# Layer 0 of a two-layer kernel rewritten: fewer VectorE and GpSimd instructions, gates kept in PSUM, a new order on every engine, and a third stack for layer 1

## The reference

```
# layer 0
ctx   = ema(x, tau_ctx)                         # h_t = a h_(t-1) + x_t
gated = x * sigmoid([x, ctx] @ Wg.T + bg)
mod   = 0.5 + sigmoid(gelu(x @ Wn1.T + bn1) @ Wn2.T + bn2)      # 32 columns
temporal = sum_d softmax(blend)[d] * ema(gated * mod[d], tau[d])  # d = 0..31
gate  = sigmoid(temporal @ Wtemp.T + btemp)
soma  = gelu(x @ Wsoma.T + bsoma)
x     = x + layernorm((soma * gate) @ Wout.T) * gamma + beta
# layer 1: 16 heads of 8 channels, each row sparse (32 listed keys) or dense with a bias
q, k, v = x @ Wq.T + bq, x @ Wk.T + bk, x @ Wv.T + bv
x = x + softmax(q k.T * scale + bias) v @ Wo.T + bo
```

## Time and profile before

| | |
|---|---|
| three runs, us | 369.98, 377.15, 368.16 |
| profiled execution, us | 366.06 |
| its span, us | 364.3 |
| granted TensorE clock, mean | 0.959 |
| busy: PE, DVE, POOL, ACT | 311.9 (86%), 296.9 (82%), 236.9 (65%), 213.2 (59%) |
| busiest groups | POOL L1411 130.1, DVE L1285 113.8, ACT L934 69.7, PE L669 69.1 |
| DMA | 18.91 MB, 192 of the issues are stack parts of 64 KB |

### The profile page before, as it was taken

How to read it: one execution, slowest core, us unless ns; L and a number is a source line. 1 busy time by engine, 2 the same in 40 slices (tenths; PEclk the granted TensorE clock), 3 DMA queues, 4 the chain that set the end, 5 groups by cost and what they waited for, 6 DMA issues and landing times. The chain is left out here.

```text
span 364.3 us, 10344 instructions
## 1 busy us (share of the span) xinstructions
PE 311.9 (86%) x3351; PEld 213.7 (59%) x3361; DVE 296.9 (82%) x1530; ACT 213.2 (59%) x452; POOL 236.9 (65%) x281
## 2 busy tenths in 40 slices
PE   1769559998999989898938499899899989999994
PEld 0425227565564746564524466777687768777772
DVE  4775997979797878879784877799799989999971
ACT  5833201565646364554705367787688868888772
POOL 2045143464655566564733497699899999999980
PEclk9969788999999999999978989999999999999998
DMA  7101000101001035100552004425544564454011
GB/s 206 48 0 31 0 0 2 30 4 29 2 0 31 3 87 94 20 0 0 74 70 32 0 4 86 91 62 71 141 102 98 82 131 104 98 78 103 3 31 30
DMA packets 23473, 18.91 MB, mean 52 GB/s; under 512 B 2304, under 2 KB 23040, under 8 KB 23424
## 3 DMA queue, kind: packets, MB, share of 16 engines
q1 hardware_dynamic: 23424, 18.31, 25.0%
HBM read 3.62 MB, written 2.10 MB: 16 GB/s over the span
## 5 line engine op out<-in xcount | busy, mean ns | idle before, releaser
L1411 POOL TENSOR_TENSOR arena<-arena,neg_max 128x512 f32<-128x512 f32 x128 | 130.1, 1050 | 21.5 <-DVE neg_max L1285 21.2
L1285 DVE CUSTOM_DVE_ANT_0 arena<-ps,arena 128x128 f32<-128x128 f32 x512 | 113.8, 286 | 13.4 <-PE ps L655 7.5
L934 ACT ACTIVATE arena<-ps 128x512 f32<-128x512 f32 x128 | 69.7, 596 | 16.3 <-PE ps L669 16.3
L669 PE MATMUL ps<-ident_sb,arena 128*128 128x128 f32 x512 | 69.1, 279 | 0.0
L1371 POOL TENSOR_TENSOR arena<-arena 128x448 f32<-128x448 f32 (+6 forms) x56 | 41.8, 746 | 29.9 <-DVE arena L1113 27.4
L669 PEld LDWEIGHTS ps<-ident_sb,arena 128*128 128x128 f32 x512 | 57.0, 142 | 6.6 <-issue 4.2
L1358 POOL TENSOR_TENSOR arena<-decay_a,arena 128x192 f32<-128x192 f32 x32 | 22.3, 717 | 38.5 <-ACT arena L794 38.5
L1285 DVE DVE_READ_ACCUMULATOR2_ANT neg_max<- 128x1 f32 x512 | 42.5, 83 | 0.0
L685 PE MATMUL ps<-arena 128*32 128x128 f32 x1024 | 41.5, 280 | 0.0
L1113 DVE TENSOR_TENSOR arena<-ps,arena 128x448 f32<-128x448 f32 (+6 forms) x56 | 23.5, 426 | 14.2 <-PE ps L456 8.7
L655 PE MATMUL ps<-arena 48*128 48x128 bf16 x512 | 25.7, 220 | 8.3 <-DVE neg_max L1285 5.7
(11 more groups left out here) (154 smaller groups left out, 594.5 us busy)
## 6 DMA issues: line engine op xcount, KB each, us to landing
arena<-q_parts SPq DMA_DIRECT2D x96, 64.0 KB
arena<-k_parts SPq DMA_DIRECT2D x96, 64.0 KB
arena<-in_x SPq DMA_DIRECT2D x8, 256.0 KB, 2.8
out<-arena SPq DMA_DIRECT2D x8, 256.0 KB, 3.0
w_sb<-in_w SPq DMA_DIRECT2D x1, 576.0 KB, 6.5
arena<-in_consts SPq DMA_DIRECT2D x1, 420.0 KB, 5.5
rows_sb<-in_rows SPq DMA_DIRECT2D x1, 288.5 KB, 3.0
ident_sb<-in_ident SPq DMA_DIRECT2D x1, 64.0 KB, 3.1
```

The source lines that it names most:

```text
L669: mm = pe.transpose(ps[1][:, q % 2, k * P:k * P + P], neg_t[q % NT_RING][:, k * P:k * P + P], ident)
L934: act.activation(probT[q % PT_RING], ps[1][:, q % 2, :], ACT.Exp, scale=-1.0)\
L1285: dve.tensor_tensor_reduce(out=neg_t[q % NT_RING][:, cs], in0=ps[0][:, score_bank(c) + slot, cs], in1=nbias[n % 2], scale=1.0, scalar=3.0e ...
L1411: pool.tensor_tensor(t4, t4, neg_max[:, n % 2, 4 * z:4 * z + 4].unsqueeze(2).broadcast_to([P, 4, P]), ALU.subtract).then_inc(s["shifted"], 1)
```

## The change

- **x twice from memory.** A transposed copy of x (`xt`, laid out on the host) is loaded straight into `xT`; `f_x` on TensorE and ScalarE goes. x is also loaded into `xb`, in place of GpSimd's x + beta; beta goes into the bias of `x1T` and into `kept`, which is added to the residual kept for the end. The values' bias goes there too, by way of Wo.
- **SyncE.** `load_x` now issues three loads: xn after the context matmuls, xT after the cross matmuls, xb after the residual, all of group m-2. There are three stacks. The third lies over xb, acc, x1g and x1T.
- **Modulation.** Wn2 is not spread over four zero-padded matrices; four matmuls of 32 rows write in two halves to two banks. VectorE's two tensor-scalars (L1089, L1090) go: ScalarE copies the tanh itself to bf16, and the constant part of 0.5 tanh + 1 becomes `lag_c`, added inside each lag product.
- **Gates in PSUM.** Both tanh activations write back into their PSUM bank, and VectorE's products read them there.
- **Values** are copied to `v_all` by ScalarE instead of VectorE.
- **Order** of every engine's step, below; the one-hots are spread over steps 0 and 1; q and k change places.
- **Prologue.** The weights come in two loads, three loads are issued by ScalarE, the lag weights are made in two halves, and two constant matmuls are new.

```diff
@@ sync
+                                   (w_sb[:, W_FIRST:, :], w[:, W_FIRST:, :], "w_rest_loaded"),
...
             def load_x(i, m):
                 sp.wait_ge(s["ctx_ps"], grp(i, m, 1, -1))
-                sp.wait_ge(s["xb_ready"], grp(i, m, 1, -1))
                 sp.dma_start(by_row(xn[m % 2]), x_v[:, group_rows(i, m), :]).then_inc(s[f"x_loaded{m % 2}"], 16)
+                sp.wait_ge(s["cross_ps"], grp(i, m, 1, -1))
+                sp.dma_start(by_row(xT[m % 2]), xt[:, group_rows(i, m), :]).then_inc(s[f"xT_loaded{m % 2}"], 16)
+                sp.wait_ge(s["x1_ready"], grp(i, m, 1, -1))
+                sp.dma_start(by_row(xb[m % 2]), x_v[:, group_rows(i, m), :]).then_inc(s[f"xb_loaded{m % 2}"], 16)
...
             sp.wait_ge(s["part3_ready"], 2)
+            sp.wait_ge(s["counts_ps"], 1)
             load_stack(0)
             sp.wait_ge(s["cross_ps"], G - 1)
             sp.wait_ge(s["part3_ready"], 4)
             load_stack(1)
-            for g in range(2, G):
-                if g >= 3:
-                    store(g - 3)
-                sp.wait_ge(s["score_ps"], NB2 * (g - 1))
-                sp.wait_ge(s["part3_ready"], 2 * (g + 1))
+            sp.wait_ge(s["v_stored"], G)
+            sp.wait_ge(s["x1b_ready"], G)
+            sp.wait_ge(s["part3_ready"], 6)
+            load_stack(2)
+            for g in range(3, G):
+                sp.wait_ge(s["score_ps"], NB2 * (g - 2))
                 load_stack(g)
+                store(g - 3)
@@ tensor
+            def constants():
+                pe.wait_ge(s["vec_step"], vec("blend_4"))
+                pe.transpose(bank(1, 0)[:, 0:P], bl_4, ident).then_inc(s["blend_turned"], 1)
+                pe.wait_ge(s["w_rest_loaded"], 16)
+                pe.matmul(bank(1, 2)[:, 0:P], col["bv"].broadcast_to([P, P]), wt["wo"], start=True, stop=True)\
+                    .then_inc(s["const_ps"], 1)
+            def lag_constants():
+                pe.wait_ge(s["vec_step"], vec("half_bw"))
+                pe.wait_ge(s["act_step"], scal("apow"))
+                pe.matmul(bank(1, 1)[:, 0:Q], half_bw[0:D, :], apow[0:D, :], start=True, stop=True)\
+                    .then_inc(s["const_ps"], 1)
             def front(i, m):
+                f_hidden(i, m)
+                f_soma(i, m)
+                f_modulation(i, m, 0)
+                f_gate_x(i, m)
+                constants()
+                f_modulation(i, m, 1)
+                f_context(i, m)          # now waits for modT_tanh
+                lag_constants()
+                f_gate_ctx(i, m)
+                f_modulation_n(i, m)
+                f_lags(i, m, range(0, 2))
+                f_gated(i, m)
+                f_lags(i, m, range(2, Q))
             def step(i, m):              # closes: from step 1 on
+                f_hidden(i, m + 1); b_carries(i, m)
+                f_modulation(i, m + 1, 0); f_gate_x(i, m + 1); f_modulation(i, m + 1, 1)
+                f_soma(i, m + 1); f_context(i, m + 1); b_locals(i, m)
+                f_modulation_n(i, m + 1); f_gate_ctx(i, m + 1); c_x1T(i, m - 1)
+                f_lags(i, m + 1, range(0, 2)); c_k(i, m - 1); b_cross(i, m)
+                f_gated(i, m + 1); c_less(i, m - 1, 1, 0); f_lags(i, m + 1, range(2, 3))
+                b_crossT(i, m); f_lags(i, m + 1, range(3, 4)); c_q(i, m - 1); b_gate(i, m)
+                c_less(i, m - 1, 1, 1); c_less(i, m - 1, 0, 0); f_lags(i, m + 1, range(4, 6))
+                c_less(i, m - 1, 0, 1); f_lags(i, m + 1, range(6, 7))
+                b_out(i, m); c_v(i, m - 1); f_lags(i, m + 1, range(7, Q))
+                # the count matmuls: end of step 1 (were: end of step 0)
@@ scalar
+                f_hidden(i, m + 1); f_modulation(i, m + 1); f_mod_part1(i, m + 1)
+                f_soma(i, m + 1); f_context(i, m + 1); f_mod_part1b(i, m + 1)
+                f_modulation_n(i, m + 1); f_gate(i, m + 1)
+                c_x1T(i, m - 1); c_part(i, m - 1, 1, 0); b_cross(i, m); f_gated(i, m + 1)
+                c_part(i, m - 1, 1, 1); c_part(i, m - 1, 0, 0); b_gate(i, m)
+                c_part(i, m - 1, 1, 2); c_part(i, m - 1, 0, 1); c_part(i, m - 1, 0, 2)
+                c_values(i, m - 1)
@@ vector
+            dve.wait_ge(s["const_ps"], 2)
+            dve.wait_ge(s["rows_loaded"], 16)
+            pro("lag_c", dve.tensor_copy(lag_c[:], bank(1, 1)[:, 0:Q]), waited=False)
...
             def f_mod_parts(i, m):
-                dve.tensor_scalar(modT[u], thd[u], 0.5, 1.0, ALU.mult, ALU.add).then_inc(s["modT_ready"], 1)
-                dve.tensor_scalar(mod_pa[u][:], thd[u], 0.5, 1.0, ALU.mult, ALU.add).then_inc(s["mod_part1"], 1)
...
             def f_lags(i, m, lags):
-                    dve.tensor_tensor(packed(prod[u][lag % 2], lag), chunks(bank(u, lag % 2), 0, Q - lag),
-                                      chunks(gT[u], 0, Q - lag), ALU.mult).then_inc(s["prod_ready"], 1)
+                    dve.scalar_tensor_tensor(packed(prod[u][lag % 2], lag), chunks(bank(u, lag % 2), 0, Q - lag),
+                                             lag_c[:, lag:lag + 1], chunks(gT[u], 0, Q - lag), ALU.add, ALU.mult)\
+                        .then_inc(s["prod_ready"], 1)
...
             def front(i, m):
+                lag_weights(0)
+                f_mod_parts(i, m)
                 f_gated(i, m)
-                f_modulation(i, m)
-                f_lags(i, m, range(Q))
+                f_lags(i, m, range(0, 2))
+                lag_weights(1)
+                f_lags(i, m, range(2, Q))
             def step(i, m):              # closes: from step 1 on; opens: steps 0 and 1
+                b_carries(i, m); c_residual(i, m - 1); neighbours()   # the last in step 0 only
+                f_mod_parts(i, m + 1); b_locals(i, m); f_gated(i, m + 1)
+                f_lags(i, m + 1, range(0, 2)); b_temporal(i, m)
+                f_lags(i, m + 1, range(2, 3)); one_hots(first, first + 4)
+                f_lags(i, m + 1, range(3, 4)); one_hots(first + 4, first + 8)
+                b_mixed(i, m); f_lags(i, m + 1, range(4, 5)); one_hots(first + 8, first + 12)
+                f_lags(i, m + 1, range(5, 6)); one_hots(first + 12, first + 16)
+                f_lags(i, m + 1, range(6, 7)); c_moments(i, m)
+                f_lags(i, m + 1, range(7, Q)); c_centre(i, m)         # then late_tables in step 1
@@ gpsimd
             def step(i, m):
-                f_inputs(i, m + 1)
+                f_decayed(i, m + 1, range(GB))
                 c_keep(i, m - 1)
-                f_accumulate(i, m + 1)
+                f_lags(i, m + 1, range(1, Q))
                 c_rstd(i, m)
```

More of the change, by code:

```diff
@@ L80, in scal, with build @@
     return ACT_STEPS.index(name) + 1
-def build(nc, x, w, wn2, cols, rows, consts, ident_in, idx, masks, out):
+def build(nc, x, xt, w, wn2, cols, rows, consts, ident_in, idx, masks, out):
     with ExitStack() as ctx:
@@ L103, in build @@
         rows_sb = sb("rows_sb", [P, R_END])
-        gamma, beta, bo, bv = [rows_sb[:, k * P:k * P + P] for k in range(4)]
+        gamma, beta, bo = [rows_sb[:, k * P:k * P + P] for k in range(3)]
         lt = sb("lt", [P, P])
@@ L159, in build @@
             xT.append(four[:, 0:W])
-            th.append(four[:, W:2 * W])
             ctxT.append(four[:, 2 * W:3 * W])
@@ L166, in build @@
             h1T.append(take(P))
-            modT.append(take(W))
             gT.append(take(W))
@@ L171, in build @@
             modn.append(take(P))
-            weights_at = at[0] - 5 * W - P
+            weights_at = at[0] - 4 * W - P
         xn = [take(W) for _ in range(2)]
-        xb, acc, x1g = [[take(W)] for _ in range(3)]
-        for bufs in (xb, acc, x1g):
-            bufs.append(take(W))
-        one_hot = arena[:, at[0]:at[0] + K_SPARSE * P // 2].bitcast(BF16).rearrange("p (j k) -> p j k", k=P)
+        third_at = at[0]
+        xb, acc, x1g = [[take(W) for _ in range(2)] for _ in range(3)]
         x1T = take(W)
+        take(W)
         def stack_at(n):
@@ L411, in f_hidden, with f_modulation @@
                                    start=True, stop=True)
                 mm.then_inc(s["h1_ps"], 1)
-            def f_modulation(i, m):
+            def f_modulation(i, m, half):
                 u = m % 2
-                pe.wait_ge(s["h1_ready"], grp(i, m, 1, 1))
-                if at_start(i, m, 1):
-                    pe.wait_ge(s["vec_step"], vec(f"wn2_row{GB - 1}"))
-                for b in range(GB):
-                    mm = pe.matmul(bank(u, 1)[:, b * P:b * P + P], wn2_row[:, b, :], h1T[u], start=True, stop=True)
-                mm.then_inc(s["modT_ps"], 1)
+                if half == 0:
+                    pe.wait_ge(s["h1_ready"], grp(i, m, 1, 1))
+                    if at_start(i, m, 1):
+                        pe.wait_ge(s["wn2_loaded"], 16)
+                    if not at_start(i, m, 2):
+                        pe.wait_ge(s["temporal_ready"], grp(i, m, 1, -1))
+                else:
+                    pe.wait_ge(s["modT_half"], grp(i, m, 1, 1))
```

(22 more changed lines are left out.)

427 lines of the change are left out of this document (222 added, 205 removed).

## The result

The kernel after takes 402.76 us (median of four runs, 398.15 to 404.77). Its ratio to the kernel before is 1.087 (95% interval 1.069 to 1.106), so it is 8.7% slower. The forecast was 376, with 385 as its upper end. The profiled execution took 402.22 us with a span of 400.3, against 364.3: 36.0 us more, where 7.1 was forecast.

A forecast was written before the change was run, and what follows sets the result against it. It took a VectorE–TensorE loop to bound the steps, and late stack loads to stall attention. Third stack landing at 249.9, 2.0 clock, the remaining time less 2.7 of waits, and 1.0 gave 371.4; rescaled, 376 us, range 364 to 385.

The forecast's parts named there:

- The sign and the mechanism: Whole kernel: slower, 376 us against 369.98, with late stack loads stalling octets 0 and 16 and a slow clock afterwards.
- Both waits and their clock: TensorE stalls 4.2 us before octet 0 and 8.8 before octet 16, then loses 2.0 to the slow clock.
- The first ends landing ... 18.1 us after its start: SyncE's stack loads: each costs 18 to 21 us; 18.1 taken for the first stack, 19.3 for the third.
- A loop between VectorE and TensorE: Steps 2 to 6: bounded by this loop with little slack, not one full engine; from 20.25 to 19.5 us each.
- Rival 3: Whole kernel longer: steps stay at 20.3, clock takes 3.4, later loads 1 us late each; 382 profiled, 4% slower; 18%.
- 0.94 us less TensorE work a step: Steps 2 to 6: TensorE drops 0.44 us of x transposes and about 0.5 of modulation matmuls, which only cover.
- The prologue (31.0, bounds up to 32.5): Before step 0: gain 1.3 us, loss 2.9, so step 0 starts at 31.0 instead of 29.45; bounds 28.5 to 32.5.
- the three loads issued by ScalarE at the start, where it waits for VectorE anyway: Start of the prologue: ScalarE's issuing of three loads costed at nothing.
- the chain to the constants: Prologue: gelus, TensorE's first half and constants, tanh and context put the constants near 16.0, where weights started at 13.51.
- the halving: Prologue: lag weights' second half, 2.95 us, sits between lag 1 and lag 2 with TensorE and GpSimd behind it.
- Steps 0 and 1: Layer 0's first two steps: sixteen one-hots, 6.0 us, move to step 1; the pair goes from 50.9 to 48.9.
- Octets 0 to 11: Attention's start: 50.2 to 48.1 us, from VectorE's carries beginning 1.35 us earlier and one copy less, 0.68.

The follow-up runs named there:

- run with small loads first: On the version with first stack early and two stacks, ScalarE's three starting loads moved to SyncE's queue behind two small ones: step 0 at 35.60 us, was 38.51.
- The table run: On the version with first stack early and two stacks: counts first among late tables, ScalarE's logarithm between q and k parts; steps 2 and 3 together 42.6 us.
- the fastest version: Kernel after with early first stack, small loads first, reordered tables, unhalved early lag weights, third stack used only when free: span 360.2 us, 0.970 of kernel before.
- the run with the halves together: On the version with first stack early and two stacks, both modulation matmul halves precede the gate's x part: steps 4 to 6 took 20.03, 20.5, 20.0 us.

## Why the forecast was wrong, step by step

**The sign and the mechanism were right.** The first stack behind SyncE's last x load, the third behind the stored values, the slow clock behind the gap (277.91 to the next scores 4.1 us at 0.50), no such wait in later groups: each is in the trace. Undoing one took its wait away and left the other (the runs with the first stack early and with two stacks). Both waits and their clock are about 26 us of the 36; I had 15. The runs won back less, 18 to 21, since two stacks bring waits of 6.1 us in later groups.

**"The first ends landing ... 18.1 us after its start" was mis-sized, and it sized both stalls.** It measured 23.7 and 24.1. For the first stack part of that is chance: the same load took 20.5 in the run with two stacks. I took the two loads of before whose ends I had rows for, the shorter for the first stack and what I called the middle for the third (the middle of 18.1 and 21.0 is 19.55, not 19.3). The trace had the other case: the load issued at 171.87 moved 71 GB/s where 1.57 MB in 18.1 us is 87, and was still going at 195. Window of the kernel before:

```profile
173.00:195.00 22.00, 15.61 (x117) 9.00 (x117) 16.38 (x53) 7.75 (x16) 12.84 (x17) 0.84 0.56 71
```

Nobody waited for it, so no wait pointed at it. The upper bound should have been 24 to 25 us, which gives stalls of 10 and 14.

**"A loop between VectorE and TensorE" was wrong as the bound of steps 2 to 6**, and with it 19.5 us. Doubling a TensorE pair costs a step 0.9 us, doubling a VectorE subtraction in the loop 0.15. Rival 3 had this part right: "steps stay at 20.3". I counted 0.94 us less TensorE work a step as cover. It did not go away. Windows of the step from 100.66 before and of the one from 130.46 after, in the columns of the earlier trace rows:

```profile
100.66:120.73 20.07, 19.04 (x140) 11.75 (x140) 16.96 (x42) 10.58 (x18) 11.78 (x15) 1.00 0.05 14
...
130.46:150.61 20.15, 19.15 (x135) 11.06 (x137) 15.64 (x40) 11.25 (x20) 9.44 (x13) 1.00 0.13 40
```

TensorE is busy 19.04 and 19.15 us. The x transposes and the padded modulation (1.44 from start to start) went and the 32-row halves came (0.84), which leaves 0.6 and not 0.94. The rest was eaten by the new order, in which groups of matmuls take longer until the next one starts: the six fp32 pairs of 512 columns together 0.4 us, and the carries, the context matmuls and the transposes together another 0.4. The timeline of TensorE, two pairs of the earlier trace rows's step and then the steady step of the kernel after:

```profile
102.87 1.02 PE L394 MATMUL ps<-arena,w_sb 128*128 128x512 f32 x2
103.73 1.02 PE L398 MATMUL ps<-arena,w_sb 128*128 128x512 f32 x2
...
132.07 0.49 PE L457 MATMUL ps<-arena,wn_sb 32*128 32x128 f32 x4
132.49 1.13 PE L422 MATMUL ps<-arena,w_sb 128*128 128x512 f32 x2
133.54 0.49 PE L457 MATMUL ps<-arena,wn_sb 32*128 32x128 f32 x4
133.96 1.13 PE L416 MATMUL ps<-arena,w_sb 128*128 128x512 f32 x2
...
147.66 0.38 PE L588 MATMUL ps<-q_parts,minus_ident_b 128*128 x1 [0.70 <-ACT q_parts L902]
```

From one pair to the next it is 0.86 us before, and 1.05 where the pair stands between two groups of 32 rows. The last row is the wait for ScalarE's q and k chain that I had named. The steady steps are 20.15, 20.65 and 20.0, the same as before; the other 4 us are steps 2 and 3 (22.5 and 22.2), which the forecast treated as steady:

```profile
88.79 1.09 PE L513 MATMUL ps<-arena 128*96 128x128 f32 x8 [2.60 <-DVE count_none L1161]
...
111.91 0.49 PE L457 MATMUL ps<-arena,wn_sb 32*128 32x128 f32 x4 [1.91 <-ACT arena L843]
```

Step 2 waits 2.60 for the counts, a wait that I had priced into step 1 and that TensorE pays in step 2; step 3 waits 1.91 for a gelu behind two table loads around the logarithm, which I had not looked at. The table run took the second one away.

**The prologue (31.0, bounds up to 32.5) failed in three terms.** First, "the three loads issued by ScalarE at the start, where it waits for VectorE anyway" were costed at nothing: ScalarE did wait, but the small loads that VectorE starts on landed 3 us later (run with small loads first: 2.9 us). Second, the chain to the constants: I let the part from the two gelus to the constants pass in 3.3 us (12.73 to 16.0), and TensorE takes 6 from the modulation to the constants (15.05 to 21.11), with pairs of 2.08 us that take 1.13 in the steps and a stand of 0.83. Third, the halving: 2.95 in the forecast for the second half, 3.8 measured, and a slow clock behind it (0.54 from 36 to 40); making the weights whole wins 1.4 us although lag 0 comes 2.5 later. Where it stands was wrong too: TensorE's lag 2 starts 2.5 us after lag 0, not some 5, and lag 4 is the one that waits. What the wait of the weights for the constants costs, which I blamed in the forecast, is not shown by itself: taken away alone it gives 0.14 us, in an execution whose context and gate matmuls ran 1.9 us longer; taken away together with ScalarE's late parts it brings lag 0 2.5 us forward and step 0 1.7.

**Steps 0 and 1** came out 1.9 us better than forecast and 3.9 below before. No run moved the one-hots back, so that it is they which pay there is read from the stages, not shown. **Octets 0 to 11** cost 3.0 more than forecast: 1.9 of that went with the wait in front of them (the run with the first stack early, where the granted clock is 0.86 instead of 0.81), whose slow clock I had not counted there. Of the 2.1 us that VectorE's early start was to give, that run shows 1.0 and the fastest version none (50.3).

**PSUM operands.** I took zero for them; the gated and the mixed product, now from PSUM, take 679 and 687 ns against 685 from SBUF. By the rule of the Trainium skill cited in the forecast (VectorE: DVE Perf Modes, The TRN2 errata) each would be longer; the trace after disagrees too. These are the groups of the kernel after by line and form:

```profile
L1239 DVE SCALAR_TENSOR_TENSOR arena<-ps,arena 128x512 f32<-128x512 f32 x8 | 5.5, 687 | 7.7 <-ACT ps L882 7.7
L1175 DVE SCALAR_TENSOR_TENSOR arena<-ps,arena 128x512 f32<-128x512 f32 x8 | 5.4, 679 | 0.0
```

## What to carry to other kernels

Before you size a new wait for a transfer, list all transfers of its kind with their rates, above all those nobody waits for, and take the slowest. To find what bounds a pipelined step, sum one engine's work from start to start before believing a chain through several engines; if the sum is nearly the step, instructions taken from other engines are worth nothing: 18 us of them in steps 2 to 6 bought nothing here. A new order can also cost the bounding engine what the removed work should have given, so price each group with its new neighbours. A load moved behind the last wait of an in-order queue is late by the whole of that wait, and memory that frees late should be given to the transfer that is needed latest, not to the next one.

## What the runs showed of the hardware that I had not expected

- 24 DMAs of 64 KB from 64 partitions to 8 take 25.3 us alone on an idle core, to 64 partitions 16.6, of which SyncE needs 15.2 to issue them. Their last piece comes 23.7 to 24.1 us after the first issue on the idle core in 19 of 24 loads, and after 17.9 to 20.0 in three of the first four loads of the kernel before.
- A 37 KB load landed 5.9 us after issue with three loads of 512 KB in all issued by ScalarE at the same time, and 2.6 us with them behind it in SyncE's own queue.
- An fp32 pair of matmuls with 512 columns took 0.86 us to the next start between groups of its own shape, 0.96 with a group of 32 rows on one side and 1.05 with one on both (the steps from 100.66 before and 130.46 after, and the run with the halves together). The pair in front of the cross matmuls took 1.05 too.
- A wait of 1.91 us on TensorE in step 3 stands in seven runs (the kernel after and six versions of it that keep the order of the tables). Half clock (2.08 us for a pair that takes 1.13) followed at once in two of them and 1 to 2 us later in two more, and not in the other three.
